# Last layer's epilogue: tanh and artanh of two maps replaced by a bounded norm, small steps moved to VectorE

## What is computed

```python
def _norm(x): return jnp.clip(jnp.linalg.norm(x, axis=-1, keepdims=True), MIN_NORM, None)
def artanh(x): return jnp.arctanh(jnp.clip(x, -1.0 + 1e-07, 1.0 - 1e-07))
def proj(x, c):          # maxnorm = 1 - 0.004
    return jnp.where(_norm(x) > maxnorm, x / _norm(x) * maxnorm, x)
def expmap0(u, c): return jnp.tanh(_norm(u)) * u / _norm(u)
def logmap0(p, c): return artanh(_norm(p)) * p / _norm(p)
...
support_t = adj @ xt
h = proj(expmap0(support_t, C_IN), C_IN)
xt = jax.nn.relu(logmap0(h, C_IN))
h = proj(expmap0(xt, C_OUT), C_OUT)
...
x = _layernorm(x + h)
```

## Time and profile before

| | us |
|---|---|
| median of 3 runs | 1886.32 |
| the profiled execution | 1889.14 |
| its span, first to last instruction | 1887.3 |
| PE busy | 1809.6 (96%) |
| ACT busy | 1023.6 (54%) |
| VectorE busy | 1208.7 (64%) |
| POOL busy | 966.1 (51%) |

### The profile page before, as it was taken

One profiled execution on the slowest core, in us unless ns is written; L12 is line 12 of the kernel. 1 busy time (PEld: TensorE's weight loads), 2 busy tenths in 40 slices (PEclk: granted clock), 3 DMA queues, 4 the chain that ended last, 5 costly groups with the idle time before them and its releaser, 6 DMA issues.

```text
span 1887.3 us, 41634 instructions
## 1 busy us (share of the span) xinstructions
PE 1809.6 (96%) x15504; PEld 1216.4 (64%) x15504; DVE 1208.7 (64%) x2246; ACT 1023.6 (54%) x1640; POOL 966.1 (51%) x1069
## 2 busy tenths in 40 slices
PE   6999999999996999999999999999999999889995
PEld 2444444444444888888888888888888888544442
DVE  4677775222226888898889889888889888201111
ACT  0110110000004888888888888888888889213323
POOL 0111110111125756778788788787887886343323
PEclk9999999999997999999999999999999999999998
DMA  9667766899987332222222232223132220869891
GB/s 377 248 231 255 261 239 230 273 372 378 401 287 212 94 93 69 86 62 89 82 80 88 72 96 75 74 85 97 58 99 77 81 85 30 323 226 319 304 317 42
DMA packets 110303, 328.78 MB, mean 174 GB/s; under 512 B 13105, under 2 KB 31281, under 8 KB 85553
## 3 DMA queue, kind: packets, MB, share of 16 engines
q1 hardware_dynamic: 87552, 285.25, 43.8%
q10 hardware_dynamic: 20016, 32.78, 4.8%
q0 software_dynamic: 2560, 8.39, 1.6%
HBM read 299.11 MB, written 27.26 MB: 173 GB/s over the span
## 4 chain that ended last, share of the span: by engine, by line
PE 48%; issue 8%; POOL 7%; ACT 3%; DVE 2%; DMA 1%; POOLq 0%; SPq 0%; DVEq 0%; ACTq 0%
PE bank L556 21%; PE bank L529 13%; PE bank L570 12%; ACT arena L780 2%; POOL arena L1322 1%; POOL small L1322 1%; DMA arena<-root_dram 1%; PE bank L426 1%; POOL arena L1315 1%; DVE arena L1108 1%; POOL small L1268 1%; POOL small L1496 0%; POOL small L1498 0%; POOL arena L1504 0%; POOL small L1481 0%
## 5 line engine op out<-in xcount | busy, mean ns | idle before, releaser
L556 PE MATMUL bank<-ident,arena 128*128 128x128 f32 x4096 | 539.3, 273 | 5.6 <-ACT arena L780 2.6
L556 PEld LDWEIGHTS bank<-ident,arena 128*128 128x128 f32 x4096 | 477.6, 140 | 82.8 <-DVE arena L1108 7.7
L780 ACT ACTIVATE arena<-arena,small 128x2048 f32<-128x2048 f32 x256 | 512.4, 2001 | 0.1
L426 PE MATMUL bank<-arena,stat_s 128*128 128x512 f32 x1016 | 448.0, 598 | 7.7 <-POOL stat_s L1322 4.9
L792 ACT ACTIVATE arena<-bank 128x512 f32<-128x512 f32 x680 | 383.0, 597 | 124.7 <-PE bank L556 122.6
L529 PE MATMUL bank<-k,parts 128*128 128x512 f32 x1024 | 371.7, 445 | 14.3 <-DMA k<-k_dram 7.0
L426 PEld LDWEIGHTS bank<-arena,stat_s 128*128 128x128 f32 x1016 | 192.5, 192 | 237.9 <-issue 230.8
L1108 DVE COPY arena<-bank 128x512 f32<-128x512 f32 x344 | 236.7, 688 | 72.8 <-PE bank L556 71.6
L1315 POOL TENSOR_SCALAR early<-arena 128x512 bf16<-128x512 f32 x128 | 246.4, 1925 | 67.1 <-DVE small L1093 27.1
L570 PE MATMUL bank<-arena,stat_x 128*32 128x128 f32 x8192 | 276.5, 276 | 0.0
L1315 POOL TENSOR_SCALAR arena<-arena 128x512 bf16<-128x512 f32 x128 | 247.3, 1932 | 42.5 <-DVE small L1093 20.3
(11 more groups left out here) (160 smaller groups left out, 1310.3 us busy)
## 6 DMA issues: line engine op xcount, KB each, us to landing
arena<-adj_cols SPq DMA_DIRECT2D x191, 1024.0 KB, 5.9
arena<-adj SPq DMA_DIRECT2D x256, 256.0 KB, 2.7
k_dram<-arena ACTq DMA_DIRECT2D x32, 256.0 KB, 7.0
q_dram<-arena ACTq DMA_DIRECT2D x32, 256.0 KB, 11.8
k<-k_dram POOLq DMA_DIRECT2D x32, 256.0 KB, 8.9
parts<-q_dram SPq DMA_DIRECT2D x128, 64.0 KB, 2.2
x_dram<-arena ACTq DMA_DIRECT2D x16, 256.0 KB, 3.7
arena<-x_dram ACTq DMA_DIRECT2D x16, 256.0 KB, 5.7
```

The source lines that it names most:

```text
L426: mm_ = pe.matmul(bank[:, to, :], stat[:, jt, :], ring[:, s, j, :], start=(jt == 0), stop=(jt == TILES - 1))
L556: last = pe.transpose(bank[:, b_, h * P:(h + 1) * P], cols[:, st % SETS, h, u * P:(u + 1) * P], ident[:, :])
L780: act.activation(cols[:, s_, h, :], cols[:, s_, h, :], ACT.Exp, bias=shift[:, t % 2, 1, i:i + 1], scale=-1.0, accum_out=blocksum[:, t % 2, ...
```

## The change

It touches `hyperbolic(c)` on ACT, VectorE and POOL. tanh, its bound and artanh of the first two maps become min(norm, atanh(1 - 0.004)). ACT makes the relu unscaled over the whole turned bank at once and keeps one set of squares and one Tanh; both logarithms, one Tanh, the scaled relu and the second set of squares go. VectorE sums the squares of the relu'd tile itself (`tensor_tensor_reduce`, four times) and takes eight small steps, with a reciprocal instead of the power; the factor comes in as a scale of the sum y, which is now four scaled adds, and "fh" on POOL goes. POOL keeps two square roots, one behind the other, and the normaliser's two steps. VectorE now waits for the residual, not POOL.

```diff
...
+ARTANH_MAX_NORM = math.atanh(MAX_NORM)
...
-        HA = Steps("agg", "uu", "tanh", "ln_a", "ln_b", "w", "ww", "tanh2")
-        HV = Steps("y", "bn6", "bn", "out")
-        HG = Steps("un", "un_max", "p", "un_inv", "fac", "wn", "wn_max", "wn_inv", "p2", "f2", "fh", "eps", "rstd")
+        HA = Steps("agg", "relu", "uu", "tanh")
+        HV = Steps("rr", "un_max", "un_inv", "fac", "ww", "wn", "wn_inv", "fw", "f2", "y", "bn6", "bn", "out")
+        HG = Steps("rr_root", "un", "eps", "rstd")
 
 
 
@@ -877,27 +879,13 @@
                 act.wait_ge(ring_multiplied, multiplied)
                 act.activation(agg_t, bank[:, from_bank, :], ACT.Copy).then_inc(hyp_act, 1)
                 act.wait_ge(hyp_pe, HP(c, "turned"))
+                act.activation(msg_t, bank[:, 1, :], ACT.Relu).then_inc(hyp_act, 1)
                 for t in range(TPC):
                     last = act.activation(y_t[:, t * P:(t + 1) * P], bank[:, 1, t * P:(t + 1) * P], ACT.Square,
                                           accum_out=s1[:, t:t + 1])
                 last.then_inc(hyp_act, 1)
-                act.wait_ge(hyp_pool, HG(c, "un_max"))
-                act.activation(t1, s2, ACT.Tanh).then_inc(hyp_act, 1)
-                act.wait_ge(hyp_pool, HG(c, "p"))
-                act.activation(t2, s3, ACT.Ln, bias=1.0, scale=1.0).then_inc(hyp_act, 1)
-                act.activation(t3, s3, ACT.Ln, bias=1.0, scale=-1.0).then_inc(hyp_act, 1)
-                act.wait_ge(hyp_pool, HG(c, "fac"))
-                for t in range(TPC):
-                    last = act.activation(msg_t[:, t * P:(t + 1) * P], bank[:, 1, t * P:(t + 1) * P], ACT.Relu,
-                                          scale=s5[:, t:t + 1])
-                last.then_inc(hyp_act, 1)
-                act.wait_ge(hyp_act, HA(c, "w"))
-                for t in range(TPC):
-                    last = act.activation(y_t[:, t * P:(t + 1) * P], msg_t[:, t * P:(t + 1) * P], ACT.Square,
-                                          accum_out=s6[:, t:t + 1])
-                last.then_inc(hyp_act, 1)
-                act.wait_ge(hyp_pool, HG(c, "wn_max"))
-                act.activation(t1, s7, ACT.Tanh).then_inc(hyp_act, 1)
+                act.wait_ge(hyp_dve, HV(c, "wn"))
+                act.activation(t1, s4, ACT.Tanh).then_inc(hyp_act, 1)
                 act.wait_ge(hyp_dve, HV(c, "out"))
                 act.dma_start(out[:, bass.ds(c * CHUNK, CHUNK)], x_new).then_inc(hyp_out, 16)
 
@@ -1222,9 +1210,38 @@
 
 
             def hyperbolic(c):
-                dve.wait_ge(hyp_pool, HG(c, "fh"))
-                dve.tensor_tensor(y_n, msg_t, res_in, ALU.add).then_inc(hyp_dve, 1)
-                dve.wait_ge(hyp_dve, HV(c, "y"))
+
+                def step(name, ins):
+                    ins.then_inc(hyp_dve, 1)
+                    dve.wait_ge(hyp_dve, HV(c, name))
+                    dve.nop(nofuse=True)
+
+                dve.wait_ge(hyp_act, HA(c, "relu"))
+                dve.nop(nofuse=True)
+                for t in range(TPC):
+                    s_ = slice(t * P, (t + 1) * P)
+                    last = dve.tensor_tensor_reduce(out=y_n[:, s_], in0=msg_t[:, s_], in1=msg_t[:, s_], scale=1.0,
+                                                    scalar=0.0, op0=ALU.mult, op1=ALU.add, accum_out=s6[:, t:t + 1])
+                step("rr", last)
+                dve.wait_ge(hyp_pool, HG(c, "un"))
+                dve.nop(nofuse=True)
+                step("un_max", dve.tensor_scalar(s2, s2, MIN_NORM, None, ALU.max))
+                step("un_inv", dve.reciprocal(s3, s2))
+                step("fac", dve.scalar_tensor_tensor(s5, s2, ARTANH_MAX_NORM, s3, ALU.min, ALU.mult))
+                step("ww", dve.tensor_tensor(s4, s6, s5, ALU.mult))
+                step("wn", dve.tensor_scalar(s4, s4, MIN_NORM, None, ALU.max))
+                step("wn_inv", dve.reciprocal(s7, s4))
+                step("fw", dve.tensor_tensor(s7, s7, s5, ALU.mult))
+                dve.wait_ge(hyp_act, HA(c, "tanh"))
+                dve.nop(nofuse=True)
+                step("f2", dve.scalar_tensor_tensor(t2, t1, MAX_NORM, s7, ALU.min, ALU.mult))
+                dve.wait_ge(hyp_in, 16 * (c + 1))
+                dve.nop(nofuse=True)
+                for t in range(TPC):
+                    s_ = slice(t * P, (t + 1) * P)
+                    last = dve.scalar_tensor_tensor(y_n[:, s_], msg_t[:, s_], t2[:, t:t + 1], res_in[:, s_],
+                                                    ALU.mult, ALU.add)
+                step("y", last)
                 norm_stats(y_n, hyp_dve, HV, c)
                 dve.wait_ge(hyp_pool, HG(c, "rstd"))
                 if not is_zero(c):
@@ -1477,32 +1494,12 @@
 
             def hyperbolic(c):
                 step = stage(hyp_pool, HG)
+                pool.wait_ge(hyp_dve, HV(c, "rr"))
+                pool.nop(nofuse=True)
+                step(c, "rr_root", pool.tensor_tensor(s6, s6, half, ALU.pow))
                 pool.wait_ge(hyp_act, HA(c, "uu"))
+                pool.nop(nofuse=True)
                 step(c, "un", pool.tensor_tensor(s2, s1, half, ALU.pow))
-                step(c, "un_max", pool.tensor_scalar(s2, s2, MIN_NORM, None, ALU.max))
-                pool.wait_ge(hyp_act, HA(c, "tanh"))
-                pool.nop(nofuse=True)
-                step(c, "p", pool.tensor_scalar(s3, t1, MAX_NORM, None, ALU.min))
-                step(c, "un_inv", pool.tensor_tensor(s5, s2, minus_one, ALU.pow))
-
-                pool.wait_ge(hyp_act, HA(c, "ln_b"))
-                pool.tensor_tensor(t2, t2, t3, ALU.subtract).then_inc(hyp_sub, 1)
-                pool.wait_ge(hyp_sub, 2 * c + 1)
-                pool.nop(nofuse=True)
-                pool.tensor_scalar(t2, t2, 0.5, None, ALU.mult).then_inc(hyp_sub, 1)
-                pool.wait_ge(hyp_sub, 2 * c + 2)
-                step(c, "fac", pool.tensor_tensor(s5, s5, t2, ALU.mult))
-                pool.wait_ge(hyp_act, HA(c, "ww"))
-                step(c, "wn", pool.tensor_tensor(s7, s6, half, ALU.pow))
-                step(c, "wn_max", pool.tensor_scalar(s7, s7, MIN_NORM, None, ALU.max))
-                step(c, "wn_inv", pool.tensor_tensor(s6, s7, minus_one, ALU.pow))
-                pool.wait_ge(hyp_act, HA(c, "tanh2"))
-                pool.nop(nofuse=True)
-                step(c, "p2", pool.tensor_scalar(t1, t1, MAX_NORM, None, ALU.min))
-                step(c, "f2", pool.tensor_tensor(s7, s6, t1, ALU.mult))
-                pool.wait_ge(hyp_in, 16 * (c + 1))
-                step(c, "fh", pool.tensor_tensor(tiles(msg_t), tiles(msg_t), s7.unsqueeze(2).to_broadcast([P, TPC, P]),
-                                                 ALU.mult))
                 pool.wait_ge(hyp_dve, HV(c, "bn"))
                 rsqrt_var(c, step)
 
```

More of the change, by code:

```diff
@@ L1 @@
+import math
 from contextlib import ExitStack
@@ L294, in build_program @@
         hyp_pe, hyp_act, hyp_dve, hyp_pool = [sem(f"hyp_{e}") for e in ("pe", "act", "dve", "pool")]
-        hyp_in, hyp_out, hyp_sub = sem("hyp_in"), sem("hyp_out"), sem("hyp_sub")
+        hyp_in, hyp_out = sem("hyp_in"), sem("hyp_out")
         HP = Steps("turned")
-        HA = Steps("agg", "uu", "tanh", "ln_a", "ln_b", "w", "ww", "tanh2")
-        HV = Steps("y", "bn6", "bn", "out")
-        HG = Steps("un", "un_max", "p", "un_inv", "fac", "wn", "wn_max", "wn_inv", "p2", "f2", "fh", "eps", "rstd")
+        HA = Steps("agg", "relu", "uu", "tanh")
+        HV = Steps("rr", "un_max", "un_inv", "fac", "ww", "wn", "wn_inv", "fw", "f2", "y", "bn6", "bn", "out")
+        HG = Steps("rr_root", "un", "eps", "rstd")
         block = ctx.enter_context(nc.Block())
```

## The result

The changed kernel takes 1880.41 us (median of 7 runs, 1879.48 to 1883.39) against 1887.03 for the kernel before in the same series (median of 7). The ratio is 0.9959, with a 95% interval of 0.995 to 0.9968: 7.7 us faster, between 6.0 and 9.4. The forecast was 1878.0 with a range of 1876.4 to 1881.0. The profiled execution took 1883.39 us, its span is 1881.5 us.

A forecast was written before the change was run, and what follows sets the result against it. PE, busy 96% of the span, was taken as the bound, so only its idle places pay: 5.75 us in the tail plus 2.54 us of stall, 8.29 off 1886.32, gives 1878.0 us, range 1876.4 to 1881.0.

The forecast's parts named there:

- What bounds the kernel: Whole kernel: PE is busy 96% of the span, so the change pays only in the tail and one PE stall.
- The old chain: Tail epilogue before the change: 13.58 us from ACT's first read of the turned tile to the row statistics (L917).
- the stall: PE waits before chunk 3's turn for ACT's late copy; 2.54 us, gone whole if the chain shortens by at least 2.5.
- The new chain: Tail epilogue after the change, priced step by step: row statistics start at 7.83 us, so the tail shrinks by 5.75 us.
- What goes at no gain: Two table loads per chunk on ACT, 1.28 us each, go; the one at L900 was called hidden anyway.
- The port lock: VectorE and GpSimd share ports; POOL idle, so small steps stay cheap; at 0.40 instead of 0.17 the chain grows 1.8 us.
- the half rate: VectorE's multiply-and-sums with two fp32 SBUF sources: by the skill's rule 0.5 us longer, kernel 1878.5; the trace disagrees for L966.
- The sum: Tail 5.75 plus stall 2.54 make 8.29 us, taken off the timed median 1886.32: 1878.0 us.
- Dear small steps: Rival, chance 0.14: VectorE's eight small steps and rr cost upper prices through a port lock or register work; 1880.4 us.
- The stall stays or moves: Rival, chance 0.05: PE waits for something else at the fourth turn, so only the tail counts; 1880.6 us.
- Nearly no change: Rival, chance 0.04: both of the two rivals before it together, or hidden joints in the chain; 1884 us.
- Slower: Rival, chance 0.03: VectorE's steps cost as much as POOL's power, 1.04 + 0.21 us instead of 0.27; 1891.7 us.

## Why the prediction was right, point by point

**What bounds the kernel.** Right. PE's busy time stood still, and the gain is where PE waited and where it had nothing left to do.

**The old chain and the stall.** Right. The stall was 2.54 us by the count of records; it went whole, 2.53 us in the profile of after and 2.59 when it was removed by itself.

**The new chain.** Right in every step. Forecast 7.83, measured 7.93. The steps: relu 0.60 (0.60). VectorE's start behind it 0.14 for 0.10. The four multiply-and-sums 0.93 (1866.53 to 1867.46) for 1.03; four with a pitch of 0.21 us. POOL's start 0.15 (0.15), its powers 1.01 each for 1.04, the gap between them 0.27 for 0.21, since the second one has a wait on ACT and a nop more. VectorE from 1869.99 to the start of the tanh 1.30 for 1.29 (1.26 and 0.03). f2 ends at 1872.22, 0.96 after L1232 has ended, for 0.89: f2 and y had 0.25 and 0.26 us of wait and nop ahead of them, where I had put 0.17. y 1.14 (1.14). No term was off by more than 0.1, and they were off both ways.

**What goes at no gain.** Half right. One table load is left in the layer, before the first tanh (1698.65 us), beside POOL's powers. The load at L900 was hidden, as I said: without it, POOL's steps from L1496 to L1501 lie as they did. But I put both loads of a chunk under this heading, and the one at L887 was on the old path, 1.28 us between the tanh and the first logarithm. With the reciprocal still on POOL only 0.99 us came of the tanh, the logarithms and this load together, because the reciprocal took their place. The sum did not suffer, since it builds the new chain up from nothing and subtracts it from the old one as measured.

**The port lock and the half rate.** The small steps stayed at 0.16 to 0.18 because POOL was idle; with POOL at work they took up to 0.90. L1223 has two fp32 sources in SBUF and a sum, and takes 0.29 us with a pitch of 0.21. I had 0.297 from the full rate; half rate would add 0.13. The Trainium skill (Vector Engine (DVE) Microarchitecture Reference, Points that are easy to get wrong) has half throughput for one instruction form with two non-bf16 sources in SBUF; L1223 shows none of it, though the trace calls it a custom operation and does not say whether it has that form.

**The sum.** The two terms hold: 8.29 was forecast, 8.18 is in the two places. The time holds less tightly. It fell by 7.7 us by the ratio (6.0 to 9.4) and by 6.6 by the medians, and against the forecast of 1878.0 the median is 2.4 higher. Of that, 0.7 is the reference, which was 1886.32 when I predicted and 1887.03 in the longer series; 0.1 is the two terms; 1.15 is the last store. What is left, 0.4 us, is within the spread of the runs. The step that did not hold is thus the sentence that from L917 on nothing changes: true for the instructions, which take 4.21 us to the issue of the store (4.20), not for the landing, which took 3.2 us instead of 2.0. The other part that the prediction took as unchanged, the time at which the layer starts, came 1.28 and 2.96 us later in the two pairs of profiles. How much of that is in the timed runs is not known. The median is 0.6 us under the upper end of my range, which had no room set aside for a later start or a later landing; that it still lies inside is in this part luck.

**The rivals.** Dear small steps: their cause exists but had no occasion. The stall stays or moves: no, as the distances of the turns show. Nearly no change: no, the chain had no hidden joints. Slower, through a step on VectorE as dear as a power on POOL: 0.27 against 1.25 us.

## What to carry to other kernels

When one engine is busy all through, look for the two places where a side chain still counts: the tail behind its last instruction, and the places where an in-order engine's copy stands behind the end of the chain before; price both from the rows and add them. Before moving small steps between VectorE and POOL, compare their prices for just these operations (a reciprocal 0.18 us against a power of 1.04) and see that the engine they leave is idle meanwhile. What a removed function saves is only what exceeds the work that lay beside it, here 0.99 us for three activations and two table loads, as long as the reciprocal stayed a power of 1.04 us on POOL.

## What the runs showed of the hardware that I had not expected

- After a wait of 5.78 us PE ran at a granted clock of 0.50 for about 5 us, 2.7 us lost on top of the wait; after one of 2.37 us it stayed at 1.00. Unused products in two waits of 5 to 6 us kept the records at their full speed.
- A power on POOL costs 1.01 us for 4 columns and 1.64 for 8, while a product costs 0.20 for 4 and 1.04 for 512.
- VectorE's steps that meet a POOL product end 0.01 to 0.02 us after it; the reciprocal does not wait.
- The last store landed 1.15 us later in the four profiles with an instruction load in the last 12 us, whose packet runs ahead of the store's last one.
